# A block of ones multiplied by itself 32 times on TensorE ahead of the first block of a two-product graph layer

## The reference

```
h = maximum(layernorm(x), 0)
B = (adj + adj.T) * 0.5 + I
d = rowsum(B) ** -0.5                 # 0 where the sum is not positive
M = d[:, None] * B * d[None, :]
out = x + (adj @ M) @ h
```

## Time and profile before

| what | us |
|---|---|
| median of three runs | 181.61 |
| lowest and highest run | 181.34, 183.07 |
| the profiled execution's own time | 181.94 |
| its span, first to last instruction | 180.2 |
| TensorE matmuls (PE) busy | 164.4, 91% of the span, 704 matmuls |
| TensorE weight loads (PEld) busy | 131.0 |
| VectorE (DVE) busy | 85.4 |
| ScalarE (ACT) busy | 77.1 |
| GpSimd (POOL) busy | 29.1 |

### The profile page before, as it was taken

One profiled execution on the slowest core, in us unless ns is written; L12 is line 12 of the kernel. 1 busy time (PEld: TensorE's weight loads), 2 busy tenths in 40 slices (PEclk: granted clock), 3 DMA queues, 4 the chain that ended last, 5 costly groups with the idle time before them and its releaser, 6 DMA issues.

```text
span 180.2 us, 1916 instructions
## 1 busy us (share of the span) xinstructions
PE 164.4 (91%) x704; PEld 131.0 (73%) x704; DVE 85.4 (47%) x140; ACT 77.1 (43%) x134; POOL 29.1 (16%) x55
## 2 busy tenths in 40 slices
PE   0029999999999999999999999999999999999992
PEld 0027888888888888886788888888888888888760
DVE  0457767888885974965054134251331513401101
ACT  4468879898995983914324023031130320100000
POOL 1125955345324610000000000000000000000000
PEclk9999999999999999999999999999999999999999
DMA  6999999988996000000013942010110101101001
GB/s 180 352 407 412 408 412 384 337 325 322 310 302 159 4 0 0 0 0 0 4 34 85 395 161 88 28 62 0 58 58 0 58 4 58 58 0 58 22 36 34
DMA packets 8745, 25.29 MB, mean 140 GB/s; under 512 B 877, under 2 KB 1133, under 8 KB 8737
## 3 DMA queue, kind: packets, MB, share of 16 engines
q1 hardware_dynamic: 8737, 25.18, 38.9%
HBM read 22.26 MB, written 2.77 MB: 139 GB/s over the span
## 4 chain that ended last, share of the span: by engine, by line
PE 91%; DMA 3%; DVE 2%; SPq 1%; ACT 1%; issue 0%
PE bank L482 91%; DMA S<-in_adj_dram 3%; SPq L164 1%; DVE ring L385 1%; ACT ring L283 1%; SPq L165 0%; ACT g L294 0%; DVE y_out L436 0%; DVE S L352 0%; SPq L160 0%; DVE g_scale L380 0%; DVE d_scale L376 0%
## 5 line engine op out<-in xcount | busy, mean ns | idle before, releaser
L482 PE MATMUL bank<-g,ring 128*128 128x512 f32 (+1 forms) x352 | 83.8, 402 | 12.2 <-ACT g L294 12.2
L482 PEld LDWEIGHTS bank<-g,ring 128*128 128x128 f32 (+1 forms) x352 | 66.3, 189 | 29.3 <-issue 12.2
L482 PE MATMUL bank<-z,ring 128*128 128x512 f32 (+1 forms) x352 | 80.8, 391 | 0.0
L482 PEld LDWEIGHTS bank<-z,ring 128*128 128x128 f32 (+1 forms) x352 | 64.7, 184 | 15.9
L301 ACT CAST ring<-AT 128x1408 fp32r<-128x1408 f32 (+1 forms) x11 | 14.6, 1324 | 47.1 <-PE bank L482 47.1
L436 DVE TENSOR_TENSOR y_out<-bank,x_res 128x512 f32<-128x512 f32 (+1 forms) x11 | 7.6, 692 | 52.1 <-PE bank L482 45.2
L420 DVE TENSOR_TENSOR ring<-AT,ring 128x1280 fp32r<-128x1280 f32 (+1 forms) x11 | 15.8, 1440 | 6.0 <-ACT ring L301 6.0
L363 DVE SCALAR_TENSOR_TENSOR S<-S,AT 128x1354 f32<-128x1354 f32 (+1 forms) x11 | 17.4, 1581 | 0.6 <-POOL S L211 0.4
L385 DVE TENSOR_TENSOR ring<-S,ring 128x1024 fp32r<-128x1024 f32 x10 | 12.3, 1233 | 7.9 <-ACT ring L283 7.9
L306 ACT ACTIVATE z<-bank,d_scale 128x512 fp32r<-128x512 f32 (+1 forms) x12 | 7.4, 693 | 14.5 <-PE bank L482 14.5
L283 ACT CAST ring<-S 128x1024 fp32r<-128x1024 f32 x11 | 11.4, 1035 | 2.5 <-DVE S L352 2.5
(11 more groups left out here) (39 smaller groups left out, 37.5 us busy)
## 6 DMA issues: line engine op xcount, KB each, us to landing
AT<-in_adj_t_dram SPq DMA_DIRECT2D x10, 677.0 KB, 6.2
S<-in_adj_dram SPq DMA_DIRECT2D x10, 677.0 KB, 7.9
x_in<-in_x_dram SPq DMA_DIRECT2D x11, 256.0 KB, 5.1
x_res<-in_x_dram SPq DMA_DIRECT2D x1, 2560.0 KB, 9.7
out_dram<-y_out SPq DMA_DIRECT2D x10, 256.0 KB
AT<-in_adj_t_dram SPq DMA_DIRECT2D x2, 256.0 KB, 3.4
S<-in_adj_dram SPq DMA_DIRECT2D x2, 256.0 KB, 4.4
AT<-in_adj_t_dram SPq DMA_DIRECT2D x1, 507.8 KB, 7.2
```

Of the source, the lines that this page charges most:

```text
L482: return nc.tensor.matmul(dst, stationary, rhs[0:r, parts[1], :], start=first, stop=final)
```

## The change

VectorE, before anything else, writes ones into one 128 x 512 tile, the head of g's last block. That tile is next written with its real content by `scale_g(X)`, long after. A new semaphore, `warm_ready`, tells TensorE. TensorE waits for it, and then multiplies the tile's first 128 columns (as the stationary operand) with all its 512 columns 32 times, each time into bank 7 and each as a product of its own. Step 0 follows; its first matmul into each bank starts a new sum, so nothing of the 32 products is left in one.

```
+    WARM = 32
...
+        warm_ready = sem("warm_ready")
...
+            nc.vector.memset(g[:, FULL, 0, :].bitcast(f32), 1.0).then_inc(warm_ready, 1)
             add_first_rows()
             degree(0)
...
+            pe.wait_ge(warm_ready, 1)
+            for _ in range(WARM):
+                nc.tensor.matmul(bank[LO - 1][:, :], g[:, FULL, 0, 0:P], g[:, FULL, 0, :], start=True, stop=True)
             for k in range(FULL):
                 step(k)
```

## The result

The changed kernel takes 180.19 us (median of 14 runs, 179.54 to 181.52), the kernel before, run beside it, 181.17 (14 runs, 180.23 to 183.07). The ratio is 0.9952, with a 95% interval of 0.9928 to 0.9975: faster by half a per cent (0.25% to 0.72%), and inside the band of 1% that the prediction held for most likely. The forecast was 180.9 and a gain of 0.94 us; the measured difference of the medians is 0.98. The median of 180.19 lies 0.11 under the low end of the range, because the median of before is also 0.44 lower over 14 runs than over the three that the forecast had. In the profiled executions the span went from 180.2 to 179.3, and the time from 181.94 to 181.06, where the sum against the profiled execution had 181.0.

What follows compares the result with a forecast made beforehand. TensorE was taken as the bound: one wait for block 0, then matmuls, the first ten distances slow. The profiled 181.94 - 0.94 gave 181.0, from the median 180.7; 180.9 us was taken, range 180.3 to 181.9.

Steps and rivals of the forecast that it cites:

- the band of 1%: Whole kernel: time within 1% (1.8 us) of the kernel before, chance 0.89; faster by more 0.06, slower by more 0.05.
- the sum against the profiled execution: Whole kernel: the profiled 181.94 us less the gain of 0.94 gives 181.0.
- What bounds the kernel: TensorE: waits once, 12.2 us for block 0's g, then no matmul waits; time lies in the distances between matmuls.
- the slow start: TensorE's first ten distances from 12.19: 4.27 us at the lower clock where 2.33 would do, costing 1.94 us.
- The memset: VectorE at the start: writing the ones takes 0.5 us, hidden by the wait for block 0; first product near 1.4.
- The 32 products: TensorE before step 0: ten slow distances take 4.27 us, 22 more 5.13; free at 10.8, the last ending near 11.0.
- Is the clock kept?: TensorE between products and step 0: 1.2 us idle should not lose the clock, kept 3.5 us at the program's end.
- the clock is lost: Rival, between the 32 products and step 0: step 0 starts slow again, time 181.6 to 181.9 us, chance 0.13.
- What is late next: Steps 1 and 2 wait for their g, starting at 18.61 and 24.38; step 2 is 0.94 us earlier; chance 0.77.
- Does the gain last?: From step 2 to the end: reserves grow, the tail step has 2.87 us, so all 0.94 us lasts.
- The size: Gain 0.94 us with ten matmuls before the clock's rise; 0.16 with 6, 1.72 with 14.
- The spread of the runs: Three runs before lie 1.73 us apart, about the slow start's cost; a little of this should go.

Runs made afterwards that it cites:

- best: Changed kernel with 36 products, scales of blocks 1 and 2 before their rests, GpSimd's block 2 power before block 3's diagonal, masks later; ratio 0.9897 to the kernel before.
- after5: The changed kernel again, nothing altered, on the chip of three follow-up kernels; ratio 0.9972 to the kernel before, span 178.3 us.
- w24: Changed kernel with 24 products of ones in place of 32; one profiled run, span 180.1 us.
- w16: Changed kernel with 16 products of ones in place of 32; one profiled run, span 181.1 us.
- w24_5: Changed kernel with 24 products in place of 32, run again and timed; ratio 0.9966 to the kernel before, span 179.0 us.
- masks: Changed kernel with only GpSimd's move: masks of the tail after the power of block 3; one profiled run, span 178.6 us.
- scales: Changed kernel with only VectorE's move: block 1's scales ahead of its rests; one profiled run, span 178.7 us.
- both: Changed kernel with GpSimd's tail masks after block 3's power and VectorE's block 1 scales ahead of its rests; ratio 0.9940 to the kernel before.
- both_cold: Kernel before with GpSimd's masks after block 3's power and VectorE's block 1 scales ahead of its rests, without products; ratio 1.0022 to the kernel before.
- w4: Changed kernel with 4 products of ones in place of 32; one profiled run, span 179.0 us.
- after: The changed kernel with 32 products, in its first profile; span 179.3 us, ratio 0.9952 to the kernel before.

## Why the prediction was right, step by step

**What bounds the kernel.** Right. One wait, then matmuls only; the 1.94 us of the slow start were there to be had: best, with the operands' chains shortened as well, starts step 2 2.00 us sooner after step 0 than the kernel before.

**The memset.** Right: it took 0.48 us where 0.5 was taken, and the first product starts at 1.50 where 1.4 was forecast. VectorE's first sum starts at 6.13, sooner than the 6.66 of before, so nothing was held up by it.

**The 32 products.** Right in size: the last starts at 11.26 - 0.40 = 10.86 and ends at 11.26, where "near 11.0" stood. In that profile the level rose after eleven products, not ten; in the second profile of this kernel (after5) the 32 took 9.34 us and not 9.76, so it rose about two matmuls sooner.

**Is the clock kept?** The outcome was right, the argument was not, so luck had a part in it. TensorE was idle for 0.95 us and the clock was kept, as in all five other profiles with 32 products (idle for up to 1.4 us). But the prediction took the 3.5 us at the end of one program as a bound from below, and w24 lost the clock after 2.7; in two other places, shown further down, it fell 2.1 us after the last matmul. Also, "the clock is lost" was priced as no gain, which is not what was measured. In w16 it costs 0.86 us against the kernel before (13.99 against 13.13), and in most of the timed runs of w24_5 with a fall it cost nothing that can be seen.

**What is late next.** Right to 0.03 us: step 1 at 18.63 (18.61), step 2 at 24.35 (24.38), no wait behind it. One reserve was read too large, without effect: the rest of g for block 1 ends at 20.03 in the trace of before (VectorE L400), and its seventeenth matmul was due at 18.61 + 16 x 0.233 = 22.34, so 2.3 us and not over 3. masks, scales and both show that the chains of blocks 1 and 2 are this bound, one behind the other, and both_cold that they were covered before.

**Does the gain last?** Right: 0.97 us at step 2, 0.89 at the start of the second product, 0.9 in the span.

**The size.** That the measured 0.98 us is within 0.04 of the 0.94 is partly luck. The interval of the ratio allows 0.5 to 1.3 us, and the second comparison (after5, 0.9972) has some 0.5 us, with 0.1 to 0.9 allowed. The forecast holds for a slow start of ten distances, as in the one trace; w4 and both_cold had eight, and from step 0 to step 2 they took 12.55 and 12.58 us, only 0.4 more than the changed kernel.

**The spread of the runs.** "A little of this spread should go": the first comparison has 2.8 us before and 2.0 after, but the second has 2.2 (35 runs) and 1.4 (12). That is a hint, no more. The Trainium skill, "TensorE: Matmul & The Clock Gate" (Part 1: The HAM clock gate), has 6, 11 or 14 matmuls ahead of the rise in one kernel. The traces agree in kind. Ahead of the first rise, counted by the long distances, were ten matmuls in before and eight in both_cold, and among the products seven in w16 and w24, nine in after5, eleven in after and fourteen in best.

## What to carry to other kernels

Before warming TensorE up, read two numbers from the trace: what its first matmuls lose by their distances, and how far ahead of its step each following operand comes. The gain is about the smaller of the two. Moving a few small instructions on the engines that make the operands can be worth as much again, once the clock is up and not sooner. Let the warm-up end right at the first real operand. With 24 products, which ended 2.2 and 2.7 us early in the two profiles, the clock fell in eight of twelve runs and the ratio was 0.9966; ending 5.4 us early cost more than no warm-up, in the one run of it; and ending 2.4 us late gave the whole gain back.

## What the runs showed of the hardware that I had not expected

**The clock's fall is not a matter of idle time alone.** It was kept over 0.95 us (after) and 2.2 us (w24_5), and fell after 2.7 us (w24) and after 4.4 to 4.6 us (w16). The end of the programs, where TensorE is idle too, gives no one figure either. The kernel before kept it for 3.5 us, but the first profile of w24 lost it after 2.1 us (line and stretches below), and that of w24_5, which had kept it over 2.2 us ahead of step 0, lost it 2.1 us after its last matmul.

```profile
95.72 80.77 PE L485 MATMUL bank<-z,ring 128*128 128x512 f32 x352
176.50:178.50 2.00, 0.00 (x0) 0.00 (x0) 0.69 (x1) 0.00 (x0) 0.00 (x0) 1.00 0.03 7
178.60:180.00 1.40, 0.00 (x0) 0.00 (x0) 0.00 (x0) 0.00 (x0) 0.00 (x0) 0.50 0.36 85
```

So in these traces an idle stretch of 2.1 us can already lose the clock, and one of 4.4 us can still keep it. What decides in between was not found. The rise varies too: it came 3.1 us after the first product in w16 and 5.9 us in best.

**Two distances for the same matmuls at the same level.** TensorE's timelines in the steps of the first product, the changed kernel, then w4:

```profile
37.26 24.43 PE L485 MATMUL bank<-g,ring 128*128 128x512 f32 x104
```

```profile
37.11 24.66 PE L485 MATMUL bank<-g,ring 128*128 128x512 f32 x107
```

(24.43 - 0.40) / 103 = 0.2333 against (24.66 - 0.40) / 106 = 0.2289. Each profile has one or the other in its steps from the third on, and one kernel can have either: 0.2333 in after and w24_5, 0.2289 in after5 and w24. w16 and w24, on one chip, differ too. Before and after, as compared first, both have 0.2333. The second product has 0.229 in all. Over the 240 matmuls of the steps the two differ by 1.06 us, as much as the change is worth, and with the length of the slow start and the arrival of block 0 this is why single spans mislead here: w4, whose step 0 starts at the lower level, has a span of 179.0, under the changed kernel's 179.3. What picks the distance was not found.
